# Second layer: where the spread row norms are read for counting, and how many buffers hold the weighed rows

## What is computed

```python
q, kk, v = (einsum('oc,bcn->bon', w, xf) for w in (wq, wk, wv))
importance = nan_to_num(sum(xf * xf, axis=1))
_, topk_idx = top_k(importance, 256)
q_sel, k_sel, v_sel = (q, kk, v) taken at topk_idx, as rows
q_sel, k_sel = layer_norm(q_sel, ln_w, ln_b), layer_norm(k_sel, ln_w, ln_b)
attn = softmax(clip(nan_to_num(q_sel @ k_sel.T * C ** -0.5), -80, 80))
out = v.at[bi, ci, idx].set((attn @ v_sel).T)
y = x + einsum('oc,bcn->bon', wo, out)
```

## Time and profile before

| | us |
|---|---|
| median of 3 runs | 2792.43 |
| lowest, highest | 2790.63, 2795.66 |
| the profiled execution | 2791.04 |
| its span | 2789.2 |
| second layer in it, from the first spread norms | 2252.7 to the end |

### The profile page before, as it was taken

One profiled execution on the slowest core, in us unless ns is written; L12 is line 12 of the kernel. 1 busy time (PEld: TensorE's weight loads), 2 busy tenths in 40 slices (PEclk: granted clock), 3 DMA queues, 4 the chain that ended last, 5 costly groups with the idle time before them and its releaser, 6 DMA issues.

```text
span 2789.2 us, 33182 instructions
## 1 busy us (share of the span) xinstructions
PE 2639.5 (95%) x11856; PEld 2192.5 (79%) x11856; DVE 2103.8 (75%) x3294; ACT 1571.9 (56%) x1930; POOL 239.1 (9%) x134
## 2 busy tenths in 40 slices
PE   6999999999999999999999999999999985989998
PEld 5788887888888888888888888888888764777776
DVE  6888768876887688778877887688768856788753
ACT  3767646764676467656765676467656732333321
POOL 1001001100100010000000000000000121000100
PEclk9999999999999999999999999999999997999999
DMA  4522241213122412231223132312122162655443
GB/s 159 170 58 76 57 125 47 80 54 125 47 79 58 125 46 81 61 118 46 84 58 118 46 88 54 118 51 83 54 87 88 53 238 103 227 198 181 172 153 143
DMA packets 154849, 279.48 MB, mean 100 GB/s; under 512 B 51776, under 2 KB 52032, under 8 KB 154176
## 3 DMA queue, kind: packets, MB, share of 16 engines
q1 hardware_dynamic: 152128, 268.98, 30.6%
q0 software_dynamic: 2560, 8.39, 0.9%
HBM read 180.04 MB, written 63.18 MB: 87 GB/s over the span
## 4 chain that ended last, share of the span: by engine, by line
PE 76%; DVE 15%; issue 4%; DMA 2%; ACT 1%; SPq 1%; POOL 0%; DVEq 0%; POOLq 0%; ACTq 0%
PE tiles L371 8%; PE tiles L372 8%; PE tiles L427 8%; PE tiles L373 8%; PE tiles L473 7%; PE tiles L450 7%; PE tiles L466 7%; PE tiles L467 7%; PE tiles L446 7%; DVE p_low L695 4%; PE tiles L1304 4%; DVE row_max L679 2%; PE tiles L1354 2%; DVE flags L1546 1%; DVE flags L1544 1%
## 5 line engine op out<-in xcount | busy, mean ns | idle before, releaser
L679 DVE TENSOR_REDUCE row_max<-tiles 128x1 f32<-128x512 f32 x1014 | 695.7, 687 | 412.5 <-PE tiles L427 407.9
L543 ACT ACTIVATE p_high<-tiles 128x1024 fp32r<-128x1024 f32 x512 | 525.8, 1027 | 616.2 <-PE tiles L450 615.5
L695 DVE TENSOR_TENSOR p_low<-p_full,p_high 128x1024 fp32r<-128x1024 f32 x512 | 667.8, 1304 | 6.0 <-ACT p_full L546 5.2
L546 ACT ACTIVATE p_full<-tiles 128x1024 f32<-128x1024 f32 x512 | 521.7, 1019 | 0.0
L427 PE MATMUL tiles<-k_high_low,q_high_high 128*128 128x512 f32 x1014 | 409.7, 404 | 7.5 <-DVE row_max L679 6.9
L466 PE MATMUL tiles<-p_high,v_high 128*128 128x512 f32 x1024 | 406.8, 397 | 2.1 <-ACT num_den L562 1.3
L467 PE MATMUL tiles<-p_high,v_low 128*128 128x512 f32 x1024 | 402.2, 393 | 0.0
L427 PEld LDWEIGHTS tiles<-k_high_low,q_high_high 128*128 128x128 f32 x1014 | 313.0, 309 | 63.6 <-DVE row_max L679 22.0
L473 PE MATMUL tiles<-p_low,v_high 128*128 128x512 f32 x1024 | 326.5, 400 | 15.5 <-DVE p_low L695 15.3
L878 POOL TENSOR_TENSOR o_normed<-num_den,o_normed 64x1024 f32<-64x1024 f32 x64 | 164.4, 2569 | 2050.1 <-DMA o_normed<-rec_rows 2050.1
L450 PE MATMUL tiles<-q_low_max,k_high_one 65*128 65x512 f32 x1024 | 325.6, 399 | 0.9 <-DMA q_low_max<-row_max_top 0.8
(11 more groups left out here) (167 smaller groups left out, 3169.9 us busy)
## 6 DMA issues: line engine op xcount, KB each, us to landing
x_tiles<-in_x SPq DMA_DIRECT2D x64, 512.0 KB, 4.8
w_high<-w_split SPq DMA_DIRECT2D x126, 256.0 KB, 2.8
w_low<-w_split SPq DMA_DIRECT2D x126, 256.0 KB, 2.9
k_high_one<-k_high_low SPq DMA_DIRECT2D x128, 128.0 KB, 2.3
q_high_high<-q_high_high SPq DMA_DIRECT2D x128, 128.0 KB, 2.3
o_normed<-rec_rows SPq DMA_DIRECT2D x64, 256.0 KB, 3.7
x<-x_tiles SPq DMA_DIRECT2D x32, 512.0 KB, 4.0
x_full<-x SPq DMA_DIRECT2D x32, 512.0 KB, 6.1
```

What stands on the lines that cost most here:

```text
L543: nc.scalar.activation(ph[:, r, :], ring[:, r, :], ACT.Exp, scale=ATT_SCALE).then_inc(s_ph, 1)
L679: nc.vector.reduce_max(mcol[:, h % 2, n, i:i + 1], max_bank(h, i, n)[:, :], AX_X).then_inc(s_mx, 1)
L695: tt(pl[:, r, :], p32[:, r, :], ph[:, r, :].bitcast(F32), ALU.subtract).then_inc(s_pl, 1)
```

## The change

The spread norms are copied by ACT out of the `rows` slot to an SBUF tensor `row_norms` (in the place of `flags`) by the new `norms_out`, and `count` reads this copy. The slot is free once it is copied (`a_rows`), and the planner holds it for 2 units instead of 12. In the first round ACT makes this copy ahead of `weights_high(0)` and `weights_high(1)`. The flags that the counting writes, of which nothing is read, now go to a part of `x_back` for the first two batches and to the second `x_changed` after that. With this, one `x_changed` is left for the weighed rows: ACT's copy of batch b waits for the scatter of batch b - 1, where it waited for that of b - 2.

By the planner's rule the holders become: for `t2(1)` `t0(1)`, for `t1(2)` `q(0)`, for `t2(2)` `t0(2)` and for `t3(2)` `qt(0)`, for `k(1)` `id(2)`, and for `s` of a full round `rows`.

```diff
-HELD = dict(t=3, w=3, rows=12, q=4, k=4, s=3, x=3)
+HELD = dict(t=3, w=3, rows=2, q=4, k=4, s=3, x=3)
...
-        sel, flags = sb("chosen", [P, NT, TOP], F32R), sb("flags", [P, N])
+        sel, norms = sb("chosen", [P, NT, TOP], F32R), sb("row_norms", [P, N])
...
-        junk = flags[:, :].bitcast(BF16).rearrange("p (i x) -> p i x", i=2)
+
+        early, late = (t.bitcast(BF16).rearrange("p (i x) -> p i x", i=2)
+                       for t in (flat(back[0][:, :, :])[:, 0:N], flat(changed[1][:, :, :])))
...
                     elif w[0] == "rows":
-                        pe.wait_ge(d_cnt, cn((("c", NT - 1), b)))
+                        pe.wait_ge(a_rows, b + 1)
...
+            def norms_out(u):
+                b = u[1]
+                act.wait_ge(s_unit, unit(u))
+                if b > 0:
+                    act.wait_ge(d_cnt, cn((("c", NT - 1), b - 1)))
+                act_(norms[:, :], slot(u), ACT.Copy).then_inc(a_rows, 1)
...
-                if b > 1:
+                if b > 0:
                     for r in range(RT):
-                        act.wait_ge(s_scat[r], 16 * (b - 1))
-                act_(flat(changed[b % 2][:, :, :]), slot(u), ACT.Copy).then_inc(a_z, 1)
+                        act.wait_ge(s_scat[r], 16 * b)
+                act_(flat(changed[0][:, :, :]), slot(u), ACT.Copy).then_inc(a_z, 1)
...
+                    elif u[0] == "rows":
+                        norms_out(u)
+                        if u[1] == 0:
+                            weights_high(0)
+                            weights_high(1)
                     elif u[0] == "w":
                         product_high(u[1])
                         if u[1] == 0:
                             last_o_high()
-                        else:
-                            weights_high(0)
-                            weights_high(1)
...
             def count(b, t):
-                src = slot(("rows", b))
+                src = norms[:, :]
                 if t == 0:
-                    dve.wait_ge(s_unit, unit(("rows", b)))
+                    dve.wait_ge(a_rows, b + 1)
                 mine = imp[:, 1, t:t + 1]
-                ones = junk[:, t % 2, :]
+                ones = (early if b < 2 else late)[:, t % 2, :]
```

More of the change, by code:

```diff
@@ L1204, in top_layer @@
             sem(n) for n in ("d_imp", "d_cnt", "d_sel", "d_id", "d_lo", "d_ln", "d_sm", "d_set", "d_row", "d_y"))
-        p_pow, d_xl = sem("p_pow"), sem("d_xl")
+        p_pow, d_xl, a_rows = sem("p_pow"), sem("d_xl"), sem("a_rows")
         a_w, d_w, s_wr, a_wqk, p_wqk, s_lnb = (
@@ L1568, in numbers @@
                 for r in range(RT):
-                    v.scalar_tensor_tensor(out=junk[:, r, 0:P], in0=src[:, r * P:(r + 1) * P], scalar=1.0,
+                    v.scalar_tensor_tensor(out=(early if b < 2 else late)[:, r, 0:P], in0=src[:, r * P:(r + 1) * P], scalar=1.0,
                                            in1=ident[:, :], op0=ALU.mult, op1=ALU.mult,
@@ L1652, in second_vector @@
             dve.wait_ge(s_load_w, 16 * 2)
-            v.tensor_scalar(flags[:, 0:P], lower[:, :], 1.0, 0.0, ALU.mult, ALU.add,
+            v.tensor_scalar(norms[:, 0:P], lower[:, :], 1.0, 0.0, ALU.mult, ALU.add,
                             accum_out=idf[:, 0:1]).then_inc(d_set, 1)
@@ L1774, in scatter @@
                     nc.gpsimd.indirect_dma_start(xtok[b % 4], bass.IndirectOffsetOnAxis(idx[:, b % 3, r:r + 1], 0),
-                                                 changed[b % 2][:, r, :], None).then_inc(s_scat[r], 16)
+                                                 changed[0][:, r, :], None).then_inc(s_scat[r], 16)
             def weights_low(i):
```

## The result

The changed kernel takes 2803.59 us (median of 9 runs, 2799.60 to 2805.11), the kernel before beside it 2794.24 us (9 runs). The ratio is 1.0033 [1.0024, 1.0043]: slower by 9.4 us, where +4.4 was forecast with 2800.8 as the upper end. The profiled execution of the changed kernel took 2803.15 us with a span of 2801.4, 12.2 us over the span of before (2789.2).

A forecast was written before the change was run, and what follows sets the result against it. Each round was taken as a block of PE work followed by a block of DVE work, tied at id. The sum +8.0 - 0.2 - 1.8 - 1.6 = +4.4 us gave a median of 2796.8 us, range 2789.0 to 2800.8.

The forecast's parts named there:

- Start, +8.0: First round of layer two: copy delay 1.07, equality instructions waiting for POOL 3.77 and 3.2; ranks 8.0 us late.
- the second race: First round, POOL's second subtraction against DVE's seventh equality: DVE taken as first, so the eighth waits 3.2 us.
- rival 1: First round: POOL ahead at its second subtraction, 9.3 us late instead of 8.0, median 2798.1 us; chance 0.24.
- Copy 0 in steady rounds, counting at the same rate: Steady rounds: ACT's copy fits at no cost; counting from SBUF gains nothing, under 1 us in all.
- Rival 5: DVE's block: equality at half rate with two SBUF inputs, 8.5 us in all, sum +12.9, 2805.3 us; chance 0.06.
- Rounds -1 and 0, -0.2 - 1.8: New slot holders shorten PE waits around t2(1) and t2(2): 0.2 us gained in round -1, 1.8 in round 0.
- Round 1, -1.6: k(1) loses its 1.76 us wait; 1.6 us taken, as the token_rows store may hold ScalarE's next copy.
- start 1.45 us earlier, which ends in a longer wait at `id` (above): 0: Steady rounds: scores take the slot of rows and start earlier, PE waits longer at id instead; 0 us.
- The last three rounds, 0: Final rounds have no rows and the same releasers or earlier ones, so no change: 0 us.
- 3: First round: equality not held up by POOL; 2794.3 us, or 2789.9 with the last writes free too; chance 0.13.
- 2: Rounds -1 to 1: slots give nothing back beyond 0.2 us, 2800.2 us; chance 0.11.
- 4: DVE counting runs at double rate from SBUF, 4.3 us a batch; sum about -19, 2773 us; chance 0.04.

The follow-up runs named there:

- the run with the equality from PSUM: Changed kernel with batch 0's equality instructions reading PSUM again, its counting still reading the copy: 2792.70 us, ratio 0.9997 to the kernel before.
- the old slots: Changed kernel with rows held for 12 units and until the counting is done, as before, copy kept: 2801.02 us, ratio 1.0020.
- the repeated one: Changed kernel measured once more, unedited, beside the kernel before on another occasion: 2803.34 us, ratio 1.0026.
- swap: e3 ahead of id in PE's full rounds: changed kernel 2781.57 us (0.9951), with batch 0 counted from PSUM 2773.50 (0.9934); kernel before 2790.46 (0.9992).
- the wait before the scores back: Changed kernel with PE waiting before the scores until DVE has made the low part of x2: 2796.90 us, ratio 1.0014.
- the pad of 1408 columns: Kernel before with an unused DVE maximum over 1408 columns ahead of choosing in rounds 1 to 5: 2803.42 us, ratio 1.0037.
- the two longer pads: Kernel before with the unused DVE maximum ahead of choosing over 1664 columns, 2805.57 us (1.0039), or 2816 columns, 2816.52 us (1.0067).

## Why the prediction was wrong, step by step

- **Start, +8.0: right in size and mechanism, with the second race called the wrong way.** Measured 8.18. The collision of the equality instruction with POOL, argued from `row_max_top` and the cast, is what happened, and the run with the equality from PSUM shows it by itself. What the Trainium skill states (SBUF — State Buffer, § SBUF: two separate sides), an exclusive lock for two SBUF inputs, is borne out by 3.86 and 4.01 us, and by the form with one input that ran on. The second race went in rival 1's form: POOL was ahead and the seventh equality waited, but only 3.67 us of the 4.45 allowed for, since DVE came 0.63 us behind POOL's start. The step "since the load's issue is later" was wrong: the load landed sooner, and ACT's second copy started 15.91 us behind the first spread norms where it had started 16.74 behind them. The terms were 0.99 + 3.52 + 3.67 for the forecast 1.07 + 3.77 + 3.2; that they add up so near to 8.0 is in part luck. In the four other profiled executions with the same start POOL was ahead as well, and `id(0)` came at 26.30 to 27.53, so 7.6 to 8.8 us late.
- **Copy 0 in steady rounds, counting at the same rate: right.** The rounds with the old slots are 56.74 to 56.80 us with the copy in them (56.8 before), and the counting forms differ by 2 to 8 ns. The Trainium skill's sentence that such a form with two SBUF sources that are not bf16 "halves throughput" (Vector Engine (DVE) Microarchitecture Reference, § 7. Points that are easy to get wrong) isn't seen: 348 ns with two SBUF inputs, and 0.34 to 0.35 us for the same instruction with one, before and in the run above. Rival 5 is out; its time, 2805.3, was near the measured one for another reason.
- **Rounds -1 and 0, -0.2 - 1.8: right in kind, a little small.** `id(0)` to `id(1)` gave back 2.89 us in the first execution and 1.95 in the repeated one; by `id(2)` it was 2.55 and 2.81 us.
- **Round 1, -1.6: right, and taken away again in one execution.** From `id(2)` to `x1`, which waits for the layer norm, it took 18.89 us instead of 20.91, 2.0 us less. In the repeated run the round kept it (52.08 us against 54.18). In the first one `id(3)` came 54.01 us behind `id(2)`. There "the one thing that may hold" held: ACT waited for the store of `token_rows` before its next copy. In the two executions `id(2)` stands at 2365.86 and 2365.82, and that copy at:

```profile
2383.49 1.02 ACT L1449 ACTIVATE token_rows<-tiles 128x1024 f32<-128x1024 f32 x1 [5.49 <-DMA token_major<-token_rows]
```

```profile
2381.50 1.02 ACT L1449 ACTIVATE token_rows<-tiles 128x1024 f32<-128x1024 f32 x1 [3.53 <-PE tiles L1281]
```

ACT is 1.99 us later, and so is DVE's `x_low` behind it (2389.01, 2387.02), with which the block that ends in `chosen` begins. PE's clock fell in the first execution as well, behind the wait for `x1`:

```profile
2384.75 1.73 PE L1291 MATMUL tiles<-identity,x_back 128*128 128x128 f32 x8 [2.30 <-DVE q_k_normed L1627]
```

1.73 us for eight that took 1.09 before and in the repeated run. But ACT was late by then, and before, the clock fell there too, 1 us behind the start of the eight. So the lost 2 us are the store's and not the clock's.
- **Steady rounds, "start 1.45 us earlier, which ends in a longer wait at `id` (above): 0": this step failed.** The bookkeeping was right to a tenth (wait forecast 2.4 us, measured 2.40 to 2.44). What was wrong is the premise that a wait moved is a wait at no cost. Two waits of 1.5 and 0.9 us, 24 us apart, became one of 2.4 us, and behind that the granted clock was 0.54 and 0.78 for two windows of 2.5 us. That is 1.4 us a round where the forecast had 0, four times in the steady stretch of the first execution (`id(4)` to `id(7)`, the last of them inside the round that follows), five in the repeated one. The trace of before held the hint: its own long waits in the fill rounds are followed by a slow PE (2271.46, eight matmuls of `id` in 2.05 us behind 4.97 us of waiting; the same eight take 1.17 us in a steady round). Closer still, its wait of 2.41 us ahead of `x1` in round 1 is followed by a clock of 0.66 over 5 us. I had used "slow clock" for round 0, but never asked of a wait that I lengthened what stands behind it.
- **The last three rounds, 0: missed too.** From `id(7)` to the end it took 147.1 us before and 146.7 with the old slots, but 148.9 to 150.4 in the runs with the fourth slot and no swap, also where the clock was up behind `id(7)` (149.4 with the wait before the scores back). The forecast had named the releasers as its reason, and the releasers are those of before. Turned `k` of round 7, before and in that run:

```profile
2715.97 1.09 PE L1330 MATMUL tiles<-identity,q_k_normed 128*128 128x128 f32 x8 [3.41 <-DVE q_k_normed L1619]
```

```profile
2719.47 1.97 PE L1332 MATMUL tiles<-identity,q_k_normed 128*128 128x128 f32 x8 [3.42 <-DVE q_k_normed L1632]
```

The same wait, and a low clock that comes earlier and stays longer behind it. That is where at least part of the 2.3 us lies. The fourth slot isn't needed for it. In the kernel before with the pad of 1408 columns, which deals three slots and has no pad behind `id(7)` and the clock up there, the same eight matmuls take as long, and the stretch to the end 148.8 us (148.6 and 150.3 with the two longer pads):

```profile
2724.62 1.97 PE L1330 MATMUL tiles<-identity,q_k_normed 128*128 128x128 f32 x8 [3.41 <-DVE q_k_normed L1619]
```

So a wait of 3.41 us ended with a shorter or a longer low stretch in the same structure, and the cause of these 2.3 us stays open.

The sum of the profiled executions, then: +8.18, -2.89, +0.34 (`id(1)` to `id(2)`), -0.34 (to `id(4)`), +4.08 (to `id(7)`), +3.26 (to the end), -0.43 (the first layer) = +12.2 us. With the +4.4 of the forecast and five times 1.4 us one gets +11.4, near this and over the +9.4 of the medians; that sum leaves out the last three rounds, so its nearness proves little. Rivals 1 and 3 disputed the start, 2 what the slots give back, 4 and 5 the rate of the counting; none put a price on the longer wait at `id`, the place on which the prediction had staked a zero.

## What to carry to other kernels

A wait of the matrix engine that a change lengthens, or makes of two shorter ones, can have a price of its own behind it: look up in the granted clock what followed the waits of that length in the trace, before it is booked at zero. The remedy is to put work there that depends on nothing (here one product unit ahead of `id`), which turned a change that costs 0.33% (0.26% in the repeat) into one that gains 0.49% (ratio 0.9951), and 0.66% with its late start mended (0.9934). And copying data from PSUM to SBUF makes an instruction with a second SBUF input liable to stand still for as long as a GpSimd instruction beside it runs; check which of them run at that time.

## What the runs showed of the hardware

- One idle stretch of PE of 2.4 us cost 1.4 us of PE time behind it at 1.2 GHz, and a stretch of 4.17 us the same 1.4 us (60.06 against 61.46 us a round).
- Adding a wait of 1.5 us 24 us ahead of the other, which shortened that one from 2.4 to 0.9 us, kept the clock up and made the kernel some 3 to 7 us faster.
- The length of PE's wait doesn't settle the clock behind it: 2.63 to 2.64 us left it up twice and brought it down twice in one execution, 3.17 us left it up once, and 2.41 us at the same place was followed by 0.66 in one execution and 1.00 in another.
- Beside a GpSimd subtraction, a DVE instruction with two SBUF inputs, with an accumulator and a bf16 output, takes 3.86 and 4.01 us instead of 0.34; the double-rate writes of `chosen` take 6.43 instead of 2.19; the accumulating form with one SBUF input isn't touched (1.01 us for 768 columns).
